# The query/key projection of a transformer layer with x's two parts in one matmul of 512 columns, its halves added at eviction

## The chip, the cores and the metric

The kernel runs on one core of one Trainium2 chip. The metric is the device time of one execution in microseconds (us); a lower time is better. Engines are named as in the profile: PE is TensorE (PEld its weight loads), ACT is ScalarE, DVE is VectorE, POOL is GpSimd, and SPq is SyncE's queue, which issues every DMA here.

## The reference, cut to what matters

One transformer layer on 128 graphs of 128 nodes with 384 features, 8 heads of 48, all in float32, with a per-graph additive bias on the scores; at the end the layer's input is added once more and the rows are normalised.

```python
q = split_heads(x @ wq + bq)
k = split_heads(x @ wk + bk)
v = split_heads(x @ wv + bv)
scores = jnp.einsum('bhqd,bhkd->bhqk', q, k) * scaling   # 48 ** -0.5
scores = scores + attn_bias[:, None, :, :]
attn = jax.nn.softmax(scores, axis=-1)
ctx = jnp.einsum('bhij,bhjd->bhid', attn, v)
attn_out = ctx.transpose(0, 2, 1, 3).reshape(b, n, d) @ wo + bo
x = _rmsnorm(x + attn_out, alpha1, gamma1)
ff = jax.nn.silu(x @ w1 + b1) @ w2 + b2
x = _rmsnorm(x + ff, alpha2, gamma2)
# outside: _layernorm(input + x)
```

## The kernel before

**Groups and slots.** The 128 graphs go in 64 groups of two (PAIR), 256 nodes a group (toks). The program is a row of slots `t`. In one slot four groups are worked on in different stages: group t-1 is projected (`g_proj`), t-2 goes through attention (`g_attn`), t-3 through the first feed-forward product (`g_ff1`), t-4 through the second and the final norms (`g_ff2`), while x of group t is transposed. Slots 4 to 64 hold both a projection and a second feed-forward product: 61 slots of one form. Every engine has its own program with the order written out by hand, and the engines meet through semaphores. Each engine takes its instructions in the order in which they are written; an instruction that waits holds up all that stand behind it on that engine.

**Products.** The large products are made from two parts of each operand, high and low (HI, LO; type fp32r), as three passes: low by high, high by low, high by high. Each pass is one matmul with its own weight load (`passes`, L412).

**The projection of queries and keys** (`project_qk`) makes six blocks of 128 output features, Q0, Q1, Q2 with wq and K0, K1, K2 with wk. A block sums over three parts of the features (kb), three passes each: nine matmuls of 256 columns. PSUM bank ps_work0 takes blocks Q0 and Q1 in its two halves, ps_work1 takes Q2 and K0, and ps_work0 again K1 and K2. `qk_done[n]` tells that bank-filling n (0, 1, 2) is complete. Only filling 2 has to wait for an eviction in the same projection: `qk_ready[0]`, that Q0 and Q1 have been taken out of ps_work0.

**Evictions.** ACT takes out Q0, Q1 (L663), Q2 (L663) and K0 (L666), adding the bias and scaling the queries; DVE takes out K1 and K2 (`keys_out`, L791). They go to qk_flat in SBUF. When all are there (`qk_ready[0..2]`), SPq issues the moves (L345), DMAs that put the heads at their partitions in qk; the scores of the next slot read qk.

**What stands around it in a slot.** PE: scores (L424), `down` (L480, 72 matmuls of 384 columns), then `project_qk`, the transposes of the probabilities (L433), the transposes of x1 (L522, into ps_work0), `project_v(0)`, context (L444, L448), `project_v(1)`, output product (L412, ps_rows), transposes of x, and `up` (L412, 108 matmuls). DVE around the projection: `norm2_and_stats(0)` (L850 to L860), `residual2(1)` (L845), `layer_norm(0)` (L864), `norm2_and_stats(1)`, `layer_norm(1)`, then `keys_out`. ACT: the exponentials, the sum of squares of y for graph 0, a table load (L707), the sum of squares for graph 1 (L645; it waits for `residual2(1)`), and only then `queries_out`. The norms go ACT (sum of squares), POOL (L369, L372, the inverse root), DVE.

**The first slots.** In slot 1 DVE waits for the rows of biases and norm factors (`rows_loaded`) before `keys_out`. In slot 2 (`early`) the projection stands ahead of the scores, and ACT and DVE split weights into high and low parts ahead of its evictions. The loads of later weights stand behind the moves on SPq.

Of the kernel before, what the change touches and what calls it, by code (L numbers as in the profile page):

```python
# [31 lines left out]
ALU = mybir.AluOpType  # L32
# [3 lines left out]
P = 128  # L36
# [13 lines left out]
def build_layer(nc, x, adj, wq, bq, wk, bk, wv, bv, wo, bo, w1, b1, w2, b2,  # L50
# [16 lines left out]
    with ctx:  # L67
# [94 lines left out]

        qk_done, qk_ready = sems("qk_done", 3), sems("qk_ready", 3)
        qk_moved = sem("qk_moved")
# [125 lines left out]
        def _(sp):  # L290
# [23 lines left out]
            def slot_program(t, parity):  # L314
# [24 lines left out]
                if live(g_proj):  # L339
                    if live(g_attn):  # L340
                        sp.wait_ge(scores_done[PAIR - 1], through(g_attn))
                    for i in range(3):
                        sp.wait_ge(qk_ready[i], through(g_proj))
                    for p0, c, to, pair, n in moves:
                        sp.dma_start(qk[to:to + n, :, pair, :], qk_flat[p0:p0 + n, :, c, :]).then_inc(qk_moved, 16)  # L345
# [59 lines left out]
        def _(pe):  # L405
# [78 lines left out]
            def project_qk(g):  # L484
                for i in range(2):
                    pe.wait_ge(xT_lo[i], through(g))
                for n, blocks in enumerate((((wq_s, 0), (wq_s, 1)), ((wq_s, 2), (wk_s, 0)),
                                            ((wk_s, 1), (wk_s, 2)))):
                    if g == 0 and n < 2:
                        pe.wait_ge(weight_split, (n + 1) * kd)  # L490

                    if n == 0 and live(g - LAG_FF1 + LAG_PROJ - 1):
                        pe.wait_ge(silu_ready[fc // 2 - 2], through(g - LAG_FF1 + LAG_PROJ - 1))
                    elif n == 0 and live(g - 1):
                        pe.wait_ge(v_ready[1], through(g - 1))
                    elif n == 1 and live(g - LAG_FF1 + LAG_PROJ - 1):
                        pe.wait_ge(silu_ready[fc // 2 - 1], through(g - LAG_FF1 + LAG_PROJ - 1))
                    elif n == 1 and live(g):
                        pe.wait_ge(xT_lo[0], through(g))
                    elif n == 2:  # L500
                        pe.wait_ge(qk_ready[0], through(g))
                    for j, (w, c) in enumerate(blocks):
                        mm = passes(ps_work[n % 2][:, j * toks:(j + 1) * toks], [
                            (lambda part, kb=kb: w[:, part, kb, c * P:(c + 1) * P],
                             lambda part, kb=kb: xT[:, part, kb, :]) for kb in range(kd)])
                    mm.then_inc(qk_done[n], 1)

            def project_v(g, b):
                if g == 0 and b == 0:
                    pe.wait_ge(weight_split, proj_units)  # L510
                pe.wait_ge(qk_ready[b + 1], through(g))
                if b == 1 and live(g + LAG_PROJ - LAG_FF1):
# [45 lines left out]
            def transpose_x1(g, parity):  # L558
# [3 lines left out]
                if live(g + LAG_FF1 - LAG_PROJ):  # L562
                    pe.wait_ge(qk_ready[2], through(g + LAG_FF1 - LAG_PROJ))
                elif live(g - 1):
                    pe.wait_ge(silu_ready[fc // 2 - 2], through(g - 1))
# [54 lines left out]
        def _(act):  # L620
# [35 lines left out]

            def queries_out(g, n):

                act.wait_ge(qk_done[n], through(g))
                if n == 0 and live(g - 1):  # L660
                    act.wait_ge(qk_moved, through(g - 1, 16 * len(moves)))
                for j, c in enumerate(((0, 1), (2,))[n]):
                    e = act.activation(qk_flat[:, Q, c, :], ps_work[n][:, j * toks:(j + 1) * toks], ACT.Identity,  # L663
                                       bias=bq_col[:, c:c + 1], scale=scale)
                if n == 1:
                    e = act.activation(qk_flat[:, K, 0, :], ps_work[1][:, toks:2 * toks], ACT.Identity,  # L666
                                       bias=bk_col[:, 0:1])
                e.then_inc(qk_ready[n], 1)

# [21 lines left out]
            def slot_program(t, parity):  # L691
# [5 lines left out]
                if early:  # L697
                    weights_hi(t, 0)
                    for n in range(2):
                        queries_out(g_proj, n)  # L700
                if live(g_attn):
# [8 lines left out]
                if live(g_proj) and not early:  # L710
                    queries_out(g_proj, 0)
                    if t == 1:
                        weights_hi(t, 0)
                    queries_out(g_proj, 1)
                if live(g_attn):
# [26 lines left out]
        def _(dve):  # L742
# [41 lines left out]

            def keys_out(g):

                dve.wait_ge(qk_done[2], through(g))
                if live(g - 1):
                    dve.wait_ge(qk_moved, through(g - 1, 16 * len(moves)))
                for c in (1, 2):  # L790
                    e = dve.tensor_scalar(qk_flat[:, K, c, :], ps_work[0][:, (c - 1) * toks:c * toks],  # L791
                                          bk_col[:, c:c + 1], None, ALU.add)
                e.then_inc(qk_ready[2], 1)

# [72 lines left out]
            def slot_program(t, parity):  # L867
# [5 lines left out]
                if early:  # L873
                    weights_lo(t, 0)
                    keys_out(g_proj)
                if live(g_attn):
# [7 lines left out]
                if live(g_ff2):  # L884
                    norm2_and_stats(g_ff2, 0)
                    residual2(g_ff2, 1, parity)
                    layer_norm(g_ff2, 0)
                    norm2_and_stats(g_ff2, 1)
                    layer_norm(g_ff2, 1)
                if live(g_proj) and not early:  # L890
                    keys_out(g_proj)
                if live(g_ff1):
# [54 lines left out]
```

## Time and profile before

| | |
|---|---|
| median of 3 runs | 2987.4 us (2986.91 to 2988.67) |
| the profiled execution | 2988.56 us, of it 2986.8 us span |
| PE busy | 2926.4 us, 98% of the span |
| DVE busy | 1970.5 us, 66% |
| ACT busy | 1443.7 us, 48% |
| POOL busy | 695.6 us, 23% |
| TensorE clock granted, mean over the span | 0.991 |

The profile page gives busy times by engine, the chain of work that ended last, and groups of instructions; the timeline gives instructions in order of time, merged where neighbours are alike. Ends of matmuls are modelled, so a busy PE is not PE at its peak: the spacing of matmuls is read from their starts. In the steady slots `down` starts every 45.42 us.

### The profile page before, as it was taken

How to read it: one execution, taken by the hardware profiler on the slowest of the kernel's cores; microseconds unless marked ns; L12 is line 12 of the kernel's file. 1: busy time of each engine (PE TensorE's matmuls, PEld its weight loads, DVE VectorE, ACT ScalarE, POOL GpSimd, SP SyncE). 2: the span in 40 equal slices, each digit the busy share in tenths (PEclk: the TensorE clock that was granted, in tenths of full speed). 3: DMA queues.
4: the chain of work that ended last, by engine and by line, in shares of the span. 5: the costliest groups of instructions: out<-in, count | busy, mean ns of one | idle time of the engine just before them, and what ended most of it. 6: DMA issues, size and time to landing. Idle time of an engine off the chain costs nothing.

```text
span 2986.8 us, 62755 instructions
## 1 busy us (share of the span) xinstructions
PE 2926.4 (98%) x25216; PEld 2874.6 (96%) x25216; DVE 1970.5 (66%) x3621; ACT 1443.7 (48%) x4263; POOL 695.6 (23%) x968
## 2 busy tenths in 40 slices
PE   6899999999999999999999999999999999999997
PEld 5899999999999999999999999999999999999997
DVE  4666666666666666666666666666666666666664
ACT  4554554544545545544545445455455445454452
POOL 0122222222222222222222222222222222222221
PEclk8999999999999999999999999999999999999998
DMA  5212112112112121121121121121211211211210
GB/s 155 68 47 68 55 47 68 49 54 68 45 58 68 35 68 56 47 68 56 47 68 51 51 68 46 56 68 37 66 56 47 68 56 47 68 52 51 63 38 17
DMA packets 155476, 171.93 MB, mean 58 GB/s; under 512 B 18609, under 2 KB 155185, under 8 KB 155185
## 3 DMA queue, kind: packets, MB, share of 16 engines
q1 hardware_dynamic: 155184, 167.91, 18.8%
q8 instruction: 200, 3.28, 0.5%
q14 instruction: 92, 0.75, 0.1%
HBM read 92.35 MB, written 25.17 MB: 39 GB/s over the span
## 4 chain that ended last, share of the span: by engine, by line
PE 96%; DVE 1%; ACT 1%; SPq 1%; issue 0%; DMA 0%; POOL 0%; POOLq 0%; ACTq 0%; DVEq 0%
PE ps_work L412 48%; PE ps_rows L480 27%; PE ps_rows L412 7%; PE ps_att L424 4%; PE ps_att L433 4%; PE ps_att L444 2%; PE ps_att L448 2%; PE ps_work L522 2%; PE ps_rows L522 1%; ACT probs L630 1%; SPq L302 0%; SPq L345 0%; DMA stage<-in_L_gnn_w 0%; DVE w_s L754 0%; DVE y L864 0%
## 5 line engine op out<-in xcount | busy, mean ns | idle before, releaser
L412 PE MATMUL ps_work<-x1T,w_s 128*128 128x256 f32 x6912 | 848.4, 283 | 8.0 <-DVE x1T L812 7.1
L412 PEld LDWEIGHTS ps_work<-x1T,w_s 128*128 128x128 f32 x6912 | 836.6, 189 | 8.6 <-DVE x1T L812 7.3
L480 PE MATMUL ps_rows<-w_s,h 128*128 128x384 f32 x4608 | 816.1, 338 | 0.0
L480 PEld LDWEIGHTS ps_rows<-w_s,h 128*128 128x128 f32 x4608 | 795.9, 188 | 7.5
L686 ACT ACTIVATE h_raw<-ps_work,b_col 128x256 f32<-128x256 f32 x768 | 321.9, 470 | 485.6 <-PE ps_work L412 485.6
L630 ACT ACTIVATE probs<-probs,neg_max 128x128 f32<-128x128 f32 x1024 | 396.1, 388 | 249.0 <-DVE neg_max L766 249.0
L834 DVE CAST h<-h_raw 128x512 fp32r<-128x512 f32 x384 | 164.7, 429 | 314.5 <-ACT h_raw L686 314.5
L836 DVE TENSOR_TENSOR h<-h_raw,h 128x512 fp32r<-128x512 f32 x384 | 359.5, 936 | 13.2
L369 POOL TENSOR_SCALAR mean_sq<-sum_sq 128x1 f32<-128x1 f32 x256 | 68.8, 269 | 984.7 <-ACT squares L645 984.7
L381 POOL TENSOR_TENSOR x_last<-x_last,rows 128x768 f32<-128x768 f32 x64 | 117.5, 1836 | 773.6 <-PE ps_att L424 773.6
L412 PE MATMUL ps_work<-wv_s,xT 128*128 128x384 f32 x1152 | 235.8, 349 | 2.9 <-DVE qk_flat L791 2.9
L412 PE MATMUL ps_work<-xT,wk_s 128*128 128x256 f32 x1728 | 217.3, 283 | 21.7 <-ACT qk_flat L663 21.7
L412 PEld LDWEIGHTS ps_work<-xT,wk_s 128*128 128x128 f32 x1728 | 210.9, 191 | 22.1 <-ACT qk_flat L663 22.1
L412 PE MATMUL ps_work<-xT,wq_s 128*128 128x256 f32 x1728 | 216.8, 283 | 4.6 <-DVE wq_s L754 2.9
L412 PEld LDWEIGHTS ps_work<-xT,wq_s 128*128 128x128 f32 x1728 | 214.3, 191 | 5.5 <-issue 3.3
L412 PE MATMUL ps_rows<-wo_s,ctxT 128*128 128x384 f32 x1152 | 213.2, 339 | 4.5 <-DVE ctxT L781 4.5
L412 PEld LDWEIGHTS ps_work<-wv_s,xT 128*128 128x128 f32 x1152 | 196.6, 188 | 15.6 <-issue 12.3
L412 PEld LDWEIGHTS ps_rows<-wo_s,ctxT 128*128 128x128 f32 x1152 | 203.2, 190 | 5.1 <-DVE ctxT L781 4.7
L645 ACT ACTIVATE squares<-x 128x384 f32<-128x384 f32 x128 | 67.4, 527 | 281.3 <-DVE x L819 281.2
L630 ACT ACTIVATION_READ_ACCUMULATOR probs<-probs,neg_max 128x1 f32 x1024 | 191.8, 187 | 0.0
L649 ACT ACTIVATE probs<-ps_att 128x1024 f32<-128x1024 f32 x128 | 124.3, 1022 | 136.5 <-PE ps_att L433 136.4
L775 DVE TENSOR_TENSOR probs<-probs,row_inv 128x512 f32<-128x512 f32 x256 | 177.2, 692 | 8.8
(75 smaller groups left out, 3441.7 us busy)
## 6 DMA issues: line engine op xcount, KB each, us to landing
qk<-qk_flat SPq DMA_DIRECT2D x384, 96.0 KB, 2.4
x_in<-in_x SPq DMA_DIRECT2D x64, 384.0 KB, 3.2
x_res<-in_x SPq DMA_DIRECT2D x64, 384.0 KB, 3.9
x_last<-in_x SPq DMA_DIRECT2D x64, 384.0 KB, 3.2
out<-y SPq DMA_DIRECT2D x64, 384.0 KB, 2.5
bias<-in_adj SPq DMA_DIRECT2D x64, 128.0 KB, 3.8
qk<-qk_flat SPq DMA_DIRECT2D x128, 64.0 KB, 2.1
stage<-in_L_gnn_w SPq DMA_DIRECT2D x24, 192.0 KB, 4.0
```

The costliest lines, as they stand in the source:

```text
L381: pool.tensor_tensor(x_last[:], x_last[:], row(GAMMA2), ALU.add).then_inc(x_last_biased, 1)
L412: mm = pe.matmul(ps_out, stationary(sta), moving(mov), start=(i == 0), stop=(i == n - 1))
L424: mm = pe.matmul(ps_att[b][:, at:at + P], qk[p0:p0 + dh, Q, c, b * P:(b + 1) * P], qk[p0:p0 + dh, K, c, b * P:(b + 1) * P], start=True, st ...
L433: mm = pe.transpose(ps_att[b][:, head * P:(head + 1) * P], probs[:, b, head, :], ident[:])
L480: mm = pe.matmul(ps_rows[b][:, 0:d], h[:, sta, m, b * P:(b + 1) * P], w2_s[:, mov, m, :], start=(m == 0 and i == 0), stop=(m == fc - 1 and ...
L522: mm = pe.transpose(ps_out[:, at:at + P], rows_in[:, b, kb * P:(kb + 1) * P], ident[:])
L630: e = act.activation(probs[:, b, head, :], probs[:, b, head, :], ACT.Exp, bias=neg_max[:, b, head:head + 1], accum_out=row_sum[:, b, head: ...
L649: act.activation(probs[:, b].rearrange("p h n -> p (h n)"), ps_att[b][:], ACT.Copy).then_inc(probsT_ready[b], 1)
L686: e = act.activation(h_raw[:, m % 2, j * toks:(j + 1) * toks], ps_work[m % 2][:, j * toks:(j + 1) * toks], ACT.Silu, bias=b1_col[:, 2 * m ...
L775: dve.tensor_tensor(probs[:, b, heads], probs[:, b, heads], row_inv[:, b, heads].unsqueeze(2).to_broadcast([P, hp, P]), ALU.mult).then_inc ...
L834: dve.tensor_copy(hi, h_raw[:, m % 2, :]).then_inc(h_hi[m], 1)
L836: dve.tensor_tensor(h[:, LO, 2 * m:2 * m + 2, :].rearrange("p c n -> p (c n)"), h_raw[:, m % 2, :], hi.bitcast(F32), ALU.subtract).then_in ...
```

## The change

Each of the six blocks now has a bank to itself in turn: ps_work0 for Q0, Q2, K1 and ps_work1 for Q1, K0, K2. For each kb there is one matmul of 512 columns, the high part of the weights against both parts of x (high in columns 0 to 255, low in 256 to 511), and one of 256 columns, the low part of the weights against the high part of x, into the first half. So a block takes six matmuls in place of nine, and 2304 columns as before. The sum of the two halves of the bank is the block.

Eviction has two steps for every block: ACT takes the first half into qk_flat with bias and scale (`projection_half`, signals `qk_half[n]`), and then DVE adds the second half, scaled, to what stands in qk_flat (`projection_out`, signals `qk_ready[n]`). Block n of 2 or more waits for `qk_ready[n - 2]`. The waits of `project_v`, of the transposes of x1 and of the moves are put on the new semaphores. On DVE the six additions are written between the norm steps.

```diff
-                    elif n == 2:
-                        pe.wait_ge(qk_ready[0], through(g))
-                    for j, (w, c) in enumerate(blocks):
-                        mm = passes(ps_work[n % 2][:, j * toks:(j + 1) * toks], [
-                            (lambda part, kb=kb: w[:, part, kb, c * P:(c + 1) * P],
-                             lambda part, kb=kb: xT[:, part, kb, :]) for kb in range(kd)])
+                    elif n >= 2:
+                        pe.wait_ge(qk_ready[n - 2], through(g))
+                    for kb in range(kd):
+                        cols = slice(c * P, (c + 1) * P)
+                        pe.matmul(ps_work[n % 2][:, 0:2 * toks].rearrange("p (a n) -> p a n", a=2),
+                                  w[:, HI, kb, cols], xT[:, :, kb, :], start=(kb == 0), stop=False)
+                        mm = pe.matmul(ps_work[n % 2][:, 0:toks], w[:, LO, kb, cols], xT[:, HI, kb, :],
+                                       start=False, stop=(kb == kd - 1))
                     mm.then_inc(qk_done[n], 1)
...
-                pe.wait_ge(qk_ready[b + 1], through(g))
+                pe.wait_ge(qk_ready[2 * kd - 1 - b], through(g))
...
-            def queries_out(g, n):
+            def projection_half(g, n):
...
+                of, c = divmod(n, kd)
+                act.activation(qk_flat[:, of, c, :], ps_work[n % 2][:, 0:toks], ACT.Identity,
+                               bias=(bq_col, bk_col)[of][:, c:c + 1],
+                               scale=(scale, 1.0)[of]).then_inc(qk_half[n], 1)
...
-                    queries_out(g_proj, 0)
                     if t == 1:
                         weights_hi(t, 0)
-                    queries_out(g_proj, 1)
+                    for n in range(2 * kd):
+                        projection_half(g_proj, n)
...
-            def keys_out(g):
+            def projection_out(g, n):
+
+                dve.wait_ge(qk_half[n], through(g))
+                of, c = divmod(n, kd)
+                dve.scalar_tensor_tensor(out=qk_flat[:, of, c, :], in0=ps_work[n % 2][:, toks:2 * toks],
+                                         scalar=(scale, 1.0)[of], in1=qk_flat[:, of, c, :], op0=ALU.mult,
+                                         op1=ALU.add).then_inc(qk_ready[n], 1)
```

ACT's order in a steady slot, from the last exponentials to the transposed probabilities. Before:

```order
L630 ACTIVATE probs,row_sum<-probs,neg_max 128x128 x16
L645 ACTIVATE squares,sum_sq2<-y 128x384
L707 ACT_TABLE_LOAD
L645 ACTIVATE squares,sum_sq2<-y 128x384
L663 ACTIVATE qk_flat<-ps_work0,bq_col 128x256 x2
L663 ACTIVATE qk_flat<-ps_work1,bq_col 128x256
L666 ACTIVATE qk_flat<-ps_work1,bk_col 128x256
L649 ACTIVATE probs<-ps_att0 128x1024
```

ACT's order at the same place in the changed kernel (its lines are numbered a little differently, L647 is the sum of squares):

```order
L706 ACT_TABLE_LOAD
L647 ACTIVATE squares,sum_sq2<-y 128x384
L665 ACTIVATE qk_flat<-ps_work0,bq_col 128x256
L665 ACTIVATE qk_flat<-ps_work1,bq_col 128x256
L665 ACTIVATE qk_flat<-ps_work0,bq_col 128x256
L665 ACTIVATE qk_flat<-ps_work1,bk_col 128x256
L665 ACTIVATE qk_flat<-ps_work0,bk_col 128x256
L665 ACTIVATE qk_flat<-ps_work1,bk_col 128x256
L651 ACTIVATE probs<-ps_att0 128x1024
```

ACT's four evictions have become six, one a block, still all behind the second sum of squares. DVE's order in a steady slot, from `residual2(1)` on. Before:

```order
L845 TENSOR_TENSOR y<-ps_rows,x 128x384
L864 TENSOR_SCALAR y<-y,mean_var,inv_std 128x384
L850 SCALAR_TENSOR_TENSOR y<-y,inv_rms,rows 128x384
L856 TENSOR_TENSOR y<-y,x_last 128x384
L858 BN_STATS stats<-y 128x6
L860 BN_AGGR mean_var<-stats 128x2
L864 TENSOR_SCALAR y<-y,mean_var,inv_std 128x384
L791 TENSOR_SCALAR qk_flat<-ps_work,bk_col 128x256 x2
```

DVE's order at the same place in the changed kernel (L788 is the addition of a block's second half):

```order
L842 TENSOR_TENSOR y<-ps_rows,x 128x384
L861 TENSOR_SCALAR y<-y,mean_var,inv_std 128x384
L788 SCALAR_TENSOR_TENSOR qk_flat<-ps_work,qk_flat 128x256 x2
L847 SCALAR_TENSOR_TENSOR y<-y,inv_rms,rows 128x384
L853 TENSOR_TENSOR y<-y,x_last 128x384
L855 BN_STATS stats<-y 128x6
L857 BN_AGGR mean_var<-stats 128x2
L788 SCALAR_TENSOR_TENSOR qk_flat<-ps_work,qk_flat 128x256 x2
L861 TENSOR_SCALAR y<-y,mean_var,inv_std 128x384
L788 SCALAR_TENSOR_TENSOR qk_flat<-ps_work,qk_flat 128x256 x2
```

The two evictions of keys behind the norms have become six additions, two by two among the norm steps of graph 1.

## Rows read from the trace of the kernel before

**Rows 1.** The page: busy time by engine, and the chain that ended last.

```profile
PE 2926.4 (98%) x25216; PEld 2874.6 (96%) x25216; DVE 1970.5 (66%) x3621; ACT 1443.7 (48%) x4263; POOL 695.6 (23%) x968
...
PE 96%; DVE 1%; ACT 1%; SPq 1%; issue 0%; DMA 0%; POOL 0%; POOLq 0%; ACTq 0%; DVEq 0%
```

**Rows 2.** Timeline of PE, steady slot: start us, us, engine, line, tiles, count.

```profile
1481.04 12.75 PE L480 MATMUL ps_rows<-w_s,h 128*128 128x384 f32 x72
...
1493.63 3.34 PE L412 MATMUL ps_work<-xT,wq_s 128*128 128x256 f32 x27
...
1496.81 3.33 PE L412 MATMUL ps_work<-xT,wk_s 128*128 128x256 f32 x27
...
1499.97 1.91 PE L433 MATMUL ps_att<-ident,probs 128*128 128x128 f32 x16
...
1507.63 3.28 PE L412 MATMUL ps_rows<-wo_s,ctxT 128*128 128x384 f32 x18
...
1510.75 0.60 PE L522 MATMUL ps_work<-ident,x_in 128*128 128x128 f32 x4
```

**Rows 3.** Timeline of ACT around the same projection.

```profile
1495.56 0.53 ACT L645 ACTIVATE squares<-y 128x384 f32<-128x384 f32 x1 [2.35 <-DVE y L845]
...
1496.08 0.82 ACT L663 ACTIVATE qk_flat<-ps_work,bq_col 128x256 f32<-128x256 f32 x2
1498.06 0.47 ACT L663 ACTIVATE qk_flat<-ps_work,bq_col 128x256 f32<-128x256 f32 x1 [1.16 <-PE ps_work L412]
```

**Rows 4.** Timeline of DVE around the same projection.

```profile
1495.00 0.52 DVE L845 TENSOR_TENSOR y<-ps_rows,x 128x384 f32<-128x384 f32 x1
1496.03 0.48 DVE L864 TENSOR_SCALAR y<-y,mean_var,inv_std 128x384 f32<-128x384 f32 x1 [0.50 <-POOL inv_std L372]
1497.22 0.62 DVE L850 SCALAR_TENSOR_TENSOR y<-y,inv_rms,rows 128x384 f32<-128x384 f32 x1 [0.71 <-POOL inv_rms L372]
...
1499.06 0.18 DVE L860 BATCH_NORM_AGGREGATE mean_var<-stats 128x2 f32<-128x6 f32 x1
...
1500.58 0.87 DVE L791 TENSOR_SCALAR qk_flat<-ps_work,bk_col 128x256 f32<-128x256 f32 x2
```

**Rows 5.** Groups of instructions by form: count, busy us, mean ns of one, idle before.

```profile
L850 DVE SCALAR_TENSOR_TENSOR y<-y,inv_rms,rows 128x384 f32<-128x384 f32 x128 | 79.2, 619 | 94.2 <-POOL inv_rms L372 94.2
...
L856 DVE TENSOR_TENSOR y<-y,x_last 128x384 f32<-128x384 f32 x128 | 71.5, 558 | 4.4
...
L812 DVE TENSOR_TENSOR x1T<-ps_rows,x1T 128x256 fp32r<-128x256 f32 x64 | 26.5, 414 | 0.0
```

**Rows 6.** Timeline, two hand-overs between engines: DVE to PE, then ACT to DVE.

```profile
20.17 0.88 DVE L791 TENSOR_SCALAR qk_flat<-ps_work,bk_col 128x256 f32<-128x256 f32 x2 [4.83 <-DMA rows<-in_L_gnn_gamma]
...
21.10 2.30 PE L412 MATMUL ps_work<-wv_s,xT 128*128 128x384 f32 x9 [2.86 <-DVE qk_flat L791]
...
1502.87 0.60 ACT L673 ACTIVATE x1T<-ps_work 128x512 fp32r<-128x512 f32 x1
...
1503.51 0.69 DVE L812 TENSOR_TENSOR x1T<-ps_work,x1T 128x512 fp32r<-128x512 f32 x1 [2.05 <-ACT x1T L673]
```

**Rows 7.** Timeline of slots 1 and 2: SPq, ACT and PE.

```profile
23.01 7.35 SPq L345 DMA_DIRECT2D qk<-qk_flat  x10
...
40.90 1.19 ACT L663 ACTIVATE qk_flat<-ps_work,bq_col 128x256 f32<-128x256 f32 x3
...
41.77 4.21 PE L412 MATMUL ps_work<-xT,wk_s 128*128 128x256 f32 x18 [9.85 <-ACT qk_flat L663]
45.91 2.16 PE L424 MATMUL ps_att<-qk 48*128 48x128 f32 x32
```

**Rows 8.** Stretches: length, busy us of each engine, PEclk (granted clock), DMA share, GB/s.

```profile
50.00:54.00 4.00, 1.51 (x10) 1.19 (x9) 3.71 (x6) 4.00 (x23) 0.00 (x0) 1.00 0.45 116
54.00:58.00 4.00, 2.02 (x13) 1.79 (x14) 1.74 (x4) 3.97 (x13) 0.00 (x0) 0.80 0.75 198
...
102.00:106.00 4.00, 3.20 (x25) 2.99 (x26) 2.84 (x7) 3.91 (x12) 2.23 (x4) 1.00 0.87 259
```

More of the change, by code:

```diff
@@ L160, in build_layer @@
         xT_lo = sems("xT_lo", 2)
-        qk_done, qk_ready = sems("qk_done", 3), sems("qk_ready", 3)
+        qk_done, qk_half = sems("qk_done", 2 * kd), sems("qk_half", 2 * kd)
+        qk_ready = sems("qk_ready", 2 * kd)
         qk_moved = sem("qk_moved")
@@ L341, in slot_program @@
                         sp.wait_ge(scores_done[PAIR - 1], through(g_attn))
-                    for i in range(3):
+                    for i in range(2 * kd):
                         sp.wait_ge(qk_ready[i], through(g_proj))
@@ L486, in project_qk @@
                     pe.wait_ge(xT_lo[i], through(g))
[L487 to L490, printed above, removed]
+                for n, (w, c) in enumerate([(wq_s, c) for c in range(kd)] + [(wk_s, c) for c in range(kd)]):
+                    if g == 0 and n % kd == 0:
+                        pe.wait_ge(weight_split, n + kd)
                     if n == 0 and live(g - LAG_FF1 + LAG_PROJ - 1):
@@ L562, in transpose_x1 @@
                 if live(g + LAG_FF1 - LAG_PROJ):
-                    pe.wait_ge(qk_ready[2], through(g + LAG_FF1 - LAG_PROJ))
+                    pe.wait_ge(qk_ready[2 * kd - 2], through(g + LAG_FF1 - LAG_PROJ))
                 elif live(g - 1):
@@ L661, in queries_out @@
                     act.wait_ge(qk_moved, through(g - 1, 16 * len(moves)))
[L662 to L668, printed above, removed]
+                of, c = divmod(n, kd)
+                act.activation(qk_flat[:, of, c, :], ps_work[n % 2][:, 0:toks], ACT.Identity,
+                               bias=(bq_col, bk_col)[of][:, c:c + 1],
+                               scale=(scale, 1.0)[of]).then_inc(qk_half[n], 1)
             def transposed_hi(g, i, ps_in, done, xT_out, ready):
@@ L698, in slot_program @@
                     weights_hi(t, 0)
-                    for n in range(2):
-                        queries_out(g_proj, n)
+                    for n in range(2 * kd):
+                        projection_half(g_proj, n)
                 if live(g_attn):
@@ L710, in slot_program @@
                 if live(g_proj) and not early:
-                    queries_out(g_proj, 0)
                     if t == 1:
                         weights_hi(t, 0)
-                    queries_out(g_proj, 1)
+                    for n in range(2 * kd):
+                        projection_half(g_proj, n)
                 if live(g_attn):
@@ L783, in context_lo @@
                                   ALU.subtract).then_inc(ctx_lo[b], 1)
-            def keys_out(g):
[L787 to L793, printed above, removed]
+            def projection_out(g, n):
[4 more added lines that the diff above has]
+                                         op1=ALU.add).then_inc(qk_ready[n], 1)
             def values_out(g, b):
@@ L874, in slot_program @@
                     weights_lo(t, 0)
-                    keys_out(g_proj)
+                    for n in range(2 * kd):
+                        projection_out(g_proj, n)
                 if live(g_attn):
@@ L887, in slot_program @@
                     layer_norm(g_ff2, 0)
+                if live(g_proj) and not early:
+                    for n in range(2):
+                        projection_out(g_proj, n)
+                if live(g_ff2):
                     norm2_and_stats(g_ff2, 1)
+                if live(g_proj) and not early:
+                    for n in range(2, 4):
+                        projection_out(g_proj, n)
+                if live(g_ff2):
                     layer_norm(g_ff2, 1)
                 if live(g_proj) and not early:
-                    keys_out(g_proj)
+                    for n in range(4, 2 * kd):
+                        projection_out(g_proj, n)
                 if live(g_ff1):
```

## The prediction

> **What bounds the kernel now.** I read the page first: PE is busy 98% of the span and makes 96% of the chain that ended last [rows 1], so whatever PE waits in a steady slot is paid in full and nothing on another engine counts unless PE waits for it. Then the timeline of PE in one slot: `down` at 1481.04, the projection at 1493.63, the transposes of the probabilities at 1499.97, with no gap between them [rows 2]. The projection takes 6.34 us for 54 matmuls of 256 columns, 0.1174 us each from start to start; `down` takes 12.59 us for 72 of 384 columns, 0.1749 us each. Last, ACT and DVE in that stretch, because the change puts both between PE and its bank. ACT takes out Q0 and Q1 from 1496.08 to 1496.90, though the bank was filled 18 matmuls after the start, at 1495.74. What keeps it is the sum of squares at 1495.56, which waits for DVE's `residual2(1)`, which starts only at 1495.00 [rows 3, 4]. PE needs the bank again at 1493.63 + 36 x 0.1174 = 1497.86, so today this lateness is hidden with 0.96 us to spare.
>
> **The matmuls.** For each kb and block three matmuls of 256 columns (0.352 us) become one of 512 and one of 256. The trace has none of 512. `down` gives 0.1749 us for 384 columns, and the output product 0.1733 (1507.63 to 1510.75 for 18) [rows 2], so 128 columns more cost 0.0559 to 0.0575 us and 512 columns, by one step more, 0.229 to 0.232. A lower end is 0.224, if the whole difference between 0.117 and 256 columns at 2.4 GHz (0.107) is a fixed part. I take 0.229, between the ends and from the output product, whose 18 matmuls stand in one row: a block is 3 x (0.229 + 0.117) = 1.04 us, six blocks 6.24 us against 6.34. The matmuls alone give back 0.1 us a slot (0.05 to 0.19).
>
> The Trainium skill ("TensorE: Matmul & The Clock Gate", Back-to-back issue gap) gives a matmul its columns over 2.4 GHz plus about 2.5 ns; by it the 18 weight loads and matmuls saved are worth 0.045 us a slot. The trace has 117 ns where that rule has 109, so the measured spacing goes into the sum.
>
> **The evictions, walked through one steady slot** (times as in the slot of rows 2, up to where they move). The new DVE instruction reads PSUM and SBUF, 256 columns, with a scalar. A two-operand one of that size with a PSUM input takes 0.414 us (lower end); with a scalar 384 columns take 0.619 (upper end); the scalar form costs 0.061 us more than the plain one at 384 (0.619 against 0.558) [rows 5]. I take 0.49, nearer the first, since the size is its size. Two independent DVE instructions start 0.08 us closer than one lasts, as L860 and L845, or the pair of L791 (0.87 us for two of 0.48) show [rows 4]. ACT's eviction of 256 columns takes 0.47 us, and two of them 0.82 [rows 3]. Hand-overs: ACT to DVE 0.04 us (1503.47 to 1503.51), DVE to PE 0.05 us (21.05 to 21.10) [rows 6], and from a filled bank to ACT 0.20 us after the next matmul's start (1497.86 to 1498.06) [rows 2, 3].
>
> - Q0 is full at 1494.67, Q1 at 1495.71. ACT is still behind its sum of squares: first halves at 1496.08 to 1496.55 and 1496.43 to 1496.90.
> - DVE adds Q0 from 1496.59 to 1497.08. `layer_norm(0)` ends at 1496.51 and is not in the way [rows 4]. Block 2 (Q2) can start at 1497.13, where PE is ready at 1495.71: **PE waits 1.42 us**. Of this, what was hidden before is used up because the bank is wanted after 12 matmuls instead of 36.
> - DVE adds Q1 from 1497.00 to 1497.49, and so `norm2_and_stats(1)` starts at 1497.41 instead of 1497.22. It ends 0.19 us later than before, at 1499.43 [rows 4]. Behind it stands the addition of Q2.
> - Q2 is full at 1498.17, its first half out at 1498.84; DVE is free for it only from 1499.35, and the addition ends at 1499.84. K1 needs that bank: it starts at 1499.89, while K0 ended at 1499.21. **PE waits 0.68 us**.
> - K0's addition ends at about 1500.40, before K2 wants its bank at 1500.93. K2 ends at 1501.97, where the projection ended at 1499.97 before.
>
> So a slot is 2.00 us longer (1.42 + 0.68 of waits, 0.10 of matmuls back). Nothing behind it is late again: the last additions end at about 1503.2, the transposes into ps_work0 stand behind 16 others that take 1.91 us [rows 2], at about 1503.7, and DVE waited 2.05 us before its next work there [rows 6]. ACT's two additional evictions and DVE's four additional instructions lie inside PE's waits or in idle time; the moves wait for the last addition, some 1.7 us later than for `keys_out` before, and are wanted more than 20 us later, in the next slot. Does the delay repeat? The start of `residual2(1)` hangs on the scores of its own slot (DVE's norms and ACT's exponentials follow them), so the wait is there in each of the 61 slots: **61 x 2.00 = 122 us**.
>
> **Slots 1 to 3.** In slot 1 block 2 now waits for an addition that stands behind DVE's wait for the rows, until 20.17 [rows 6]. Four blocks, partly at the 1.2 GHz level, then end at about 28 us; the moves, which began at 23.01 [rows 7], begin at about 28.8, and with them slip the weight loads behind them and the evictions of slot 2 (40.90): 5.8 us. In slot 2 PE had 18 matmuls left when the eviction came, 4.14 us from 41.77 to 45.91, at the 1.2 GHz level [rows 7], and slot 3 has one more such place, so that there are two; now it has four blocks, some 6.3 us if the clock recovers halfway, and the addition of 0.5 us ahead: 2.6 us more in each. Sum 11 us; 5 if the slip of the moves is hidden, 16 if the four blocks run at that level throughout. The profiled execution took 2988.56 us, 1.2 above the median, and the sum goes on the median: 2987.4 + 122 + 11 = **3120 us**.
>
> **Rivals.**
> - *Only the turn of the bank counts.* If ACT and DVE were at hand, the way round (0.20 + 0.47 + 0.04 + 0.49 + 0.05 = 1.25 us) against the other bank's block (1.04) leaves 0.21 us of wait at four blocks, 0.84 - 0.10 = 0.74 us a slot: 2987 + 45 + 11 = 3043 us. For it: it would hold if the sum of squares came ahead of the projection's start. Against it: ACT is seen at it until 1496.08 [rows 3].
> - *The lag heals itself* (the other side). A longer slot would let DVE and ACT arrive earlier against PE in the next one. If `residual2(1)` came 1.4 us earlier relative to the projection and DVE kept the two waits for POOL clear of it, the matmuls' saving alone would stay: 61 x 0.1, or 6 us, 2981 us, and at most 2992 with the start. It decides at a lead of 1.4 us. Against it: the sum of squares waited 2.35 us for DVE [rows 3], and DVE's work there starts from this slot's scores, not from the last slot.
> - *The clock falls.* Two waits in a slot may bring PE down to 1.2 GHz. In the start, with 1.51 and 2.02 us of work in two stretches of 4, the granted clock went from 1.00 to 0.80; with 3.20 us of work in 4 it stayed at 1.00 [rows 8]. Here the stretch from 1495.7 to 1499.9 would have 2.1 us of work and 2.1 of waits, between these. A fall costs at least what 18 matmuls lose at the lower level, 4.14 - 2.11 = 2.0 us [rows 2, 7]: 61 x 2.0 = 122, or 3242 us. The Trainium skill ("TensorE: Matmul & The Clock Gate", A second HAM failure mode: psum-queue depth-cycling) tells of just this, a kernel whose short idle times at the turn of PSUM banks make the clock swing. Whether pauses of 1.4 and 0.7 us do it, no run here shows yet.
> - *The matmul of 512 is slower than its columns*, as it reads x in two pieces of 256. At 0.26 us each, block 0, 1 and 3 still lie inside the same waits, and only K1 and K2 count: 6 x 0.03 x 61 = 11 us. This lies inside the range.
>
> **How the numbers follow.** The forecast has a chance of 0.80, the fall of the clock 0.10, the turn of the bank alone 0.06, the healing lag 0.04. The forecast's own bounds: with DVE's addition at 0.414 us both waits shrink together by 0.19 us a slot, 12 us; at 0.62 they grow by 0.4, 24 us; the start gives -6 and +5, the long matmul +11. Not all at once: 3092 to 3156 us. The other cases hold 0.20 together and stay outside. Faster or slower by over 0.2% (6 us) is about what a measurement of this kernel can tell from no change: faster 0.03, within 0.01, slower 0.96.
>
> **What would show it.** In a steady slot: PE's projection over about 8.3 us instead of 6.34, with waits for DVE's qk_flat ahead of Q2 (1.4 us) and K1 (0.7 us) and none ahead of K0 and K2; DVE's first addition right behind ACT's first half, which itself starts as its sum of squares ends; `norm2_and_stats(1)` between the second and third additions; slots every 47.4 us. Q2 waiting 0.2 us would speak for the bank's turn alone, no wait for the healing lag, and a granted clock under 1.00 in the steady stretch for the clock. The forecast is wrong if `down` starts every 45.3 us or every 49.

## The result, and the profile after

The changed kernel takes 3110.4 us (median of 4 runs, 3109.3 to 3111.7) where the kernel before, run beside it, takes 2988.0 (median of 4): 122.4 us slower, a ratio of 1.0412 with an interval of 1.0399 to 1.0425. The prediction was 3120 us, range 3092 to 3156.

From the page: busy time by engine and the chain that ended last, against [rows 1].

```profile
PE 2954.0 (95%) x24064; PEld 2818.5 (91%) x24064; DVE 2061.5 (66%) x3877; ACT 1511.5 (49%) x4391; POOL 695.9 (22%) x968
...
PE 56%; DVE 18%; ACT 17%; issue 6%; POOL 2%; DMA 1%; SPq 0%; POOLq 0%; ACTq 0%; DVEq 0%
```

PE has 1152 matmuls fewer, but the chain no longer stays on PE: it goes over ACT and DVE for a third of the span. That share is not the time lost, for PE is still busy 95% of the span: at each of PE's waits the chain turns to what released it and follows that engine's work back, over additions and norm steps to the exponentials (ACT probs L632 alone are 13% of the chain). The way there can be read in one steady slot. Timeline of PE, with the first matmul of each block (Q0, Q1, Q2, K0, K1, K2), against [rows 2]:

```profile
1605.24 0.39 PE L504 MATMUL ps_work<-xT,wq_s 128*128 128x512 f32 x1
1605.47 0.28 PE L506 MATMUL ps_work<-xT,wq_s 128*128 128x256 f32 x1
...
1606.29 0.39 PE L504 MATMUL ps_work<-xT,wq_s 128*128 128x512 f32 x1
...
1608.66 0.50 PE L504 MATMUL ps_work<-xT,wq_s 128*128 128x512 f32 x1 [1.17 <-DVE qk_flat L788]
1608.99 0.28 PE L506 MATMUL ps_work<-xT,wq_s 128*128 128x256 f32 x1
...
1609.81 0.39 PE L504 MATMUL ps_work<-xT,wk_s 128*128 128x512 f32 x1
...
1611.26 0.50 PE L504 MATMUL ps_work<-xT,wk_s 128*128 128x512 f32 x1 [0.25 <-DVE qk_flat L788]
...
1612.41 0.39 PE L504 MATMUL ps_work<-xT,wk_s 128*128 128x512 f32 x1
...
1613.45 1.91 PE L434 MATMUL ps_att<-ident,probs 128*128 128x128 f32 x16
```

An undisturbed block takes 1.05 us (1605.24 to 1606.29). Q2 could start at 1607.33 and starts at 1608.66, 1.33 us late; K1 could start at 1610.86 and starts at 1611.26, 0.40 late. After each wait the step from the first matmul to the second is 0.33 or 0.34 us in place of 0.23; I call this the restart. K0 and K2 do not wait. The projection lasts 8.21 us instead of 6.34.

Timeline of ACT and then of DVE there, against [rows 3, 4]:

```profile
1607.17 0.52 ACT L647 ACTIVATE squares<-y 128x384 f32<-128x384 f32 x1 [2.35 <-DVE y L842]
...
1607.69 0.82 ACT L665 ACTIVATE qk_flat<-ps_work,bq_col 128x256 f32<-128x256 f32 x2
1610.01 0.48 ACT L665 ACTIVATE qk_flat<-ps_work,bq_col 128x256 f32<-128x256 f32 x1 [1.50 <-PE ps_work L506]
```

```profile
1608.18 0.79 DVE L788 SCALAR_TENSOR_TENSOR qk_flat<-ps_work,qk_flat 128x256 f32<-128x256 f32 x2
1608.89 0.61 DVE L847 SCALAR_TENSOR_TENSOR y<-y,inv_rms,rows 128x384 f32<-128x384 f32 x1
...
1610.71 0.18 DVE L857 BATCH_NORM_AGGREGATE mean_var<-stats 128x2 f32<-128x6 f32 x1
1610.81 0.39 DVE L788 SCALAR_TENSOR_TENSOR qk_flat<-ps_work,qk_flat 128x256 f32<-128x256 f32 x1
1611.55 0.42 DVE L788 SCALAR_TENSOR_TENSOR qk_flat<-ps_work,qk_flat 128x256 f32<-128x256 f32 x1 [0.35 <-ACT qk_flat L665]
```

Read it as a relay: the sum of squares keeps ACT until 1607.69, the first half of Q0 goes out, DVE adds from 1608.18, PE starts Q2 at 1608.66. And Q2's first half is out at 1610.49, but DVE is in its norm steps until 1610.8, adds then, and PE starts K1 at 1611.26.

How much this is in all slots stands in one row of each kernel: the 4608 matmuls of `down`, with their first and last start. The first of them is in slot 4, ahead of the first steady projection; between the first and the last lie all 61 steady projections. The kernel before, then the changed one (the columns behind the count are the shortest, median and longest duration in ns, then the first and last start in us):

```profile
L480 PE MATMUL ps_rows<-w_s,h x4608: 333/336/444, 118.3 to 2977.9; 128*128 128x384 f32 x192
```

```profile
L481 PE MATMUL ps_rows<-w_s,h x4608: 335/336/444, 126.4 to 3100.3; 128*128 128x384 f32 x192
```

The start is 8.1 us later; between first and last lie 2973.9 us in place of 2859.6, 114.3 more or 1.874 us for each of the 61. Together 122.4 us, the whole of the difference. The experiments below are read in the same way, as **start** (first of these matmuls against 118.3) and **steady** (excess per projection over 2859.6/61).

The granted clock did not fall: it is 1.00 over the stretch from 126 to 3000 us, which holds the steady slots. Stretches of PE in the waits, columns as in [rows 8]; the first holds Q2's wait, the last is laid from one wait over the other:

```profile
1605.20:1609.20 4.00, 2.83 (x17) 2.26 (x16) 3.33 (x9) 1.34 (x4) 1.58 (x4) 1.00 0.00 0
...
1607.30:1611.30 4.00, 2.58 (x15) 1.87 (x13) 3.40 (x8) 1.94 (x6) 1.38 (x5) 1.00 0.01 3
```

### The profile page after: what moved, and what is told of

It reads as the page before. It is cut to its first block, busy times and chain, and to the rows that moved or that the text cites. A ratio compares the mean times of both kernels' runs of the same rounds, so it can differ in the third digit from the quotient of the medians.

```text
span 3109.3 us, 60837 instructions
## 1 busy us (share of the span) xinstructions
PE 2954.0 (95%) x24064; PEld 2818.5 (91%) x24064; DVE 2061.5 (66%) x3877; ACT 1511.5 (49%) x4391; POOL 695.9 (22%) x968
## 4 chain that ended last, share of the span: by engine, by line
PE 56%; DVE 18%; ACT 17%; issue 6%; POOL 2%; DMA 1%; SPq 0%; POOLq 0%; ACTq 0%; DVEq 0%
PE ps_work L413 34%; ACT probs L632 13%; PE ps_rows L413 6%; PE ps_work L504 4%; PE ps_att L434 4%; DVE neg_max L765 3%; DVE probs L761 3%; DVE y L847 2%; DVE stats L855 2%; DVE y L853 2%; DVE qk_flat L788 2%; PE ps_att L445 2%; PE ps_att L449 2%; PE ps_work L524 2%; ACT h_raw L685 2%
## 5 line engine op out<-in xcount | busy, mean ns | idle before, releaser
L632 ACT ACTIVATE probs<-probs,neg_max 128x128 f32<-128x128 f32 x1024 | 395.8, 388 | 245.0 <-DVE neg_max L765 245.0
L504 PE MATMUL ps_work<-xT,wq_s 128*128 128x512 f32 x576 | 217.0, 411 | 107.9 <-DVE qk_flat L788 103.2
L504 PEld LDWEIGHTS ps_work<-xT,wq_s 128*128 128x128 f32 x576 | 110.0, 191 | 148.5 <-DVE qk_flat L788 123.4
L788 DVE SCALAR_TENSOR_TENSOR qk_flat<-ps_work,qk_flat 128x256 f32<-128x256 f32 x384 | 157.1, 419 | 131.9 <-ACT qk_flat L665 122.8
L504 PE MATMUL ps_work<-xT,wk_s 128*128 128x512 f32 x576 | 216.0, 409 | 15.4 <-DVE qk_flat L788 15.4
L413 PEld LDWEIGHTS ps_work<-wv_s,xT 128*128 128x128 f32 x1152 | 196.6, 188 | 13.8 <-issue 13.7
L647 ACT ACTIVATE squares<-x 128x384 f32<-128x384 f32 x128 | 67.3, 526 | 281.7 <-DVE x L816 281.6
L632 ACT ACTIVATION_READ_ACCUMULATOR probs<-probs,neg_max 128x1 f32 x1024 | 191.8, 187 | 0.0
L396 POOL TENSOR_TENSOR x<-x,rows 128x768 f32<-128x768 f32 x64 | 118.2, 1847 | 288.0 <-PE ps_rows L524 288.0
```

The lines of the kernel that those rows point to most:

```text
L396: pool.tensor_tensor(x1[:, 1 - parity], x1[:, 1 - parity], row(B2), ALU.add).then_inc(x1_b2_ready, 1)
L413: mm = pe.matmul(ps_out, stationary(sta), moving(mov), start=(i == 0), stop=(i == n - 1))
L504: pe.matmul(ps_work[n % 2][:, 0:2 * toks].rearrange("p (a n) -> p a n", a=2), w[:, HI, kb, cols], xT[:, :, kb, :], start=(kb == 0), stop=F ...
L632: e = act.activation(probs[:, b, head, :], probs[:, b, head, :], ACT.Exp, bias=neg_max[:, b, head:head + 1], accum_out=row_sum[:, b, head: ...
L788: dve.scalar_tensor_tensor(out=qk_flat[:, of, c, :], in0=ps_work[n % 2][:, toks:2 * toks], scalar=(scale, 1.0)[of], in1=qk_flat[:, of, c, ...
```

## Experiments

| kernel | median us | ratio to before (interval) | start, us | steady, us a projection |
|---|---|---|---|---|
| the changed kernel | 3110.4 | 1.0412 (1.0399 to 1.0425) | +8.1 | +1.87 |
| e1_dve_order | 3149.1 | 1.0542 (1.0526 to 1.0558) | +5.4 | +2.52 |
| e2_q0_first | 3108.1 | 1.0405 (1.0388 to 1.0422) | +6.7 | +1.84 |
| e3_both_orders | 3085.7 | 1.0331 (1.0315 to 1.0346) | +8.8 | +1.49 |
| e7_e1_keys_before_norm | 3093.4 | 1.0355 (1.0339 to 1.0372) | +6.5 | +1.61 |
| e6_e3_keys_before_norm | 3029.4 | 1.0140 (1.0122 to 1.0158) | +7.5 | +0.57 |
| e4_no_addition | 2984.8 | 0.9991 (0.9981 to 1.0000) | +0.1 | -0.08 |
| e5_rows_wait_later | 3104.7 | 1.0393 (1.0379 to 1.0408) | +2.6 | +1.87 |
| c1_three_passes_spare_bank | 2978.9 | 0.9973 (0.9963 to 0.9983) | -9.4 | 0.00 |
| f1_six_banks | 2973.8 | 0.9958 (0.9945 to 0.9970) | -10.4 | -0.08 |
| f2_six_banks_rows_later | 2975.4 | 0.9960 (0.9946 to 0.9973) | -6.6 | -0.09 |

A start is not known to a microsecond. Up to the first `down`, e1, e2, e3, e6 and e7 have the same order of instructions on every engine as the changed kernel, and yet their starts run from +5.4 to +8.8; a difference of some 3 us between two starts says nothing. The steady part does not have this spread.

The question of the first three: is each wait set by the order on ACT and DVE, so that taking one away only uncovers the next (theory A in the expectations), or are the waits independent?

**e2_q0_first: Q0 ahead on ACT (first piece) and on DVE (second piece).**

```diff
+                if live(g_proj) and live(g_ff2):
+                    projection_half(g_proj, 0)
                 if live(g_ff2):
                     sum_of_squares(g_ff2, 1, y[:, 1, :], res2_ready, sum_sq2, sq2_ready)
...
                     residual2(g_ff2, 1, parity)
+                    if live(g_proj):
+                        projection_out(g_proj, 0)
                     layer_norm(g_ff2, 0)
```

> ACT takes Q0's first half ahead of the second sum of squares, and DVE adds Q0 ahead of the first layer norm; all else as in the changed kernel. Theory A: Q2 starts at about 1607.5 instead of 1608.66 in the slot read, its wait falls from 1.33 to 0.2 us; but the addition of Q2 still stands behind the norm steps, which end when they did, so K1 starts at 1611.2 as before and its wait grows from 0.4 to about 1.5 us. The slot stays at 47.3 us: 3108 to 3110 us. Rival (the two waits are independent and add up): 61 x 1.1 = 67 us less, 3043 us.

Measured 3108.1 us. Its PE timeline, blocks Q2, K0 and K1:

```profile
1557.88 0.50 PE L504 MATMUL ps_work<-xT,wq_s 128*128 128x512 f32 x1
...
1559.03 0.48 PE L504 MATMUL ps_work<-xT,wk_s 128*128 128x512 f32 x1
...
1561.58 0.50 PE L504 MATMUL ps_work<-xT,wk_s 128*128 128x512 f32 x1 [1.25 <-DVE qk_flat L790]
```

The projection starts at 1555.61, so Q2 could start at 1557.70 and is 0.18 us late instead of 1.33. K1 could start at 1560.17 and is 1.41 late instead of 0.40. The two waits are 1.59 us together where they were 1.73, K0 has a slow first matmul too, and the projection lasts 8.17 us against 8.21: the wait moved, as theory A says, and the rival's 3043 us is out.

**e1_dve_order: the additions of Q2 and K0 ahead of the norm steps.**

```diff
                 if live(g_proj) and not early:
-                    for n in range(2):
+                    for n in range(4):
                         projection_out(g_proj, n)
                 if live(g_ff2):
                     norm2_and_stats(g_ff2, 1)
-                if live(g_proj) and not early:
-                    for n in range(2, 4):
-                        projection_out(g_proj, n)
                 if live(g_ff2):
                     layer_norm(g_ff2, 1)
```

> DVE's additions of Q2 and K0 stand ahead of the second norm steps instead of behind them; all else as in the changed kernel. Theory A (each wait is the latest of ACT's and DVE's in-order work): K1 no longer waits for the norm steps but for its bank's own way round; its block starts at about 1611.0 instead of 1611.26 in the slot read, Q2's wait of 1.33 us stays. Slot 47.04 us instead of 47.30, in all 61 x 0.26 = 16 us less: 3094 us. Rival (the bank's turn alone sets the waits, the order does not matter): 3110 us, unchanged.

Measured 3149.1 us, 39 slower than the changed kernel where 16 faster was expected: a miss. PE and then DVE behind the projection:

```profile
1582.16 1.91 PE L434 MATMUL ps_att<-ident,probs 128*128 128x128 f32 x16
1584.78 0.63 PE L524 MATMUL ps_work<-ident,x 128*128 128x128 f32 x4 [0.71 <-DVE qk_flat L788]
```

```profile
1582.69 0.18 DVE L857 BATCH_NORM_AGGREGATE mean_var<-stats 128x2 f32<-128x6 f32 x1
1583.82 0.48 DVE L861 TENSOR_SCALAR y<-y,mean_var,inv_std 128x384 f32<-128x384 f32 x1 [0.95 <-POOL inv_std L373]
1584.22 0.75 DVE L788 SCALAR_TENSOR_TENSOR qk_flat<-ps_work,qk_flat 128x256 f32<-128x256 f32 x2
```

The projection itself (1574.22 to 1582.16) lasts 7.94 us, 0.27 less than in the changed kernel, as expected (K1 starts 1.19 us after K0 instead of 1.45). But the norm steps now run later on DVE, `layer_norm(1)` behind them waits 0.95 us for POOL, and behind that stand the additions of K1 and K2. The transposes of x1 go into ps_work0, K1's bank, and wait: 2.62 us after the transposes of the probabilities, where 1.75 is usual. I had worked the expectation out as far as the end of the projection and not to the next user of the bank.

**e3_both_orders: e1 and e2 together.**

> Both changes of order together. Theory A: Q2 waits 0.2 us, K1 about 0.13, each with 0.1 us of restart, the projection takes about 6.8 us instead of 8.2; slot 45.9 us, in all 61 x 1.4 = 85 us less: 3025 us, of which 8 us over the kernel before are the first slots and 29 us the turn of the bank. Rival (effects add): the sum of what the two gave alone.

Measured 3085.7 us. The projection was near what was expected (6.9 us instead of 8.2), but the same wait of the transposes stood behind it (1553.73, then 1556.36). So the gain was 25 us and not 85. The rival's sum fails too: alone the two gave -2 and +39 us, together -25.

**e6 and e7: the additions of K1 and K2 ahead of `layer_norm(1)`,** on top of e3 and of e1:

```diff
-                if live(g_ff2):
-                    layer_norm(g_ff2, 1)
                 if live(g_proj) and not early:
                     for n in range(4, 2 * kd):
                         projection_out(g_proj, n)
+                if live(g_ff2):
+                    layer_norm(g_ff2, 1)
```

> The kernel with both changes of order, and the additions of K1 and K2 ahead of layer_norm(1) instead of behind it. In its trace K1's addition stood behind a layer norm that waits 0.95 us for POOL, and PE waited for it ahead of the transposes into ps_work0 (2.63 us from the transposes of the probabilities to those of x1, where 1.75 is usual). If that is the whole of what the first expectation missed, the slot falls from 46.92 by 0.88 to 46.04 us and the time from 3085.7 by 61 x 0.88 = 54 us to 3032. Rival (something else behind the projection is late as well, DVE's splits or the values): above 3045 us.

> The kernel with only the second change of order (additions of Q2 and K0 ahead of the norm steps), and the additions of K1 and K2 ahead of layer_norm(1). The wait ahead of the transposes into ps_work0 (2.62 us where 1.75 is usual) goes: slot 47.94 - 0.87 = 47.07 us, 3149.1 - 53 = 3096 us, 15 us under the changed kernel, as was first expected of that change alone. Rival: above 3110 us.

Measured 3029.4 and 3093.4 us, against 3032 and 3096. This settles what the first expectations had missed: to within 3 us it was that one wait. With the order mended, e7's 3093 is also what e1 was first expected to give (3094), and e6's 3029 what e3 was (3025). e6 has the best order with two banks of those run: still 42 us over the kernel before, 0.57 us a projection. Its PE timeline, the first matmuls of Q2, K0 (with its second), K1, K2 and the transposes:

```profile
1520.46 0.50 PE L504 MATMUL ps_work<-xT,wq_s 128*128 128x512 f32 x1
...
1521.60 0.50 PE L504 MATMUL ps_work<-xT,wk_s 128*128 128x512 f32 x1
1521.94 0.28 PE L506 MATMUL ps_work<-xT,wk_s 128*128 128x256 f32 x1
...
1522.79 0.50 PE L504 MATMUL ps_work<-xT,wk_s 128*128 128x512 f32 x1
...
1523.94 0.49 PE L504 MATMUL ps_work<-xT,wk_s 128*128 128x512 f32 x1
...
1525.09 1.91 PE L434 MATMUL ps_att<-ident,probs 128*128 128x128 f32 x16
```

All four blocks start with a slow first matmul, 1.14 to 1.19 us apart where 1.05 is free. The way round (PE, ACT, DVE, PE) takes 0.20 + 0.47 + 0.04 + 0.42 + 0.05 = 1.18 us in these traces and does not fit behind one block. Of the 0.57 us, 0.40 are the four restarts, 0.23 real waits (0.18 ahead of Q2), and 0.07 come back from the matmuls. Not all of it is the turn of the bank: K0's restart hangs on the order too, since ACT takes Q1's first half only at 1520.63, behind the sum of squares, where the bank was full at 1520.28.

**e4_no_addition: the matmuls by themselves.** `projection_out` does nothing, `projection_half` signals `qk_ready[n]`, Q0's half ahead of the sum of squares as in e2.

> The six additions on DVE are left out (the product of the high weights with the low part of x is computed but not added), ACT's first half alone frees the bank, and Q0's stands ahead of the second sum of squares. It prices the fused matmuls by themselves. Theory A: no wait in a steady slot, the projection takes 6 x 1.045 = 6.27 us against 6.34 in the kernel before, slot 45.35 us: 4 us less than the kernel before in the steady slots, about 4 us more in the first ones, 2988 us (2983 to 2993). Rival (the matmul of 512 columns or the finer turn of the bank itself costs time): above 3000 us.

Measured 2984.8 us, at the edge of what can be told from the kernel before, and inside the expectation. A steady projection is 0.08 us shorter than before (0.07 expected); the start costs 0.1 instead of the 4 I had put down. So the fused matmuls are no slower than their columns say, and nothing of the 122 us comes from them; it comes with the way in which the banks are emptied. How much of that is the addition alone e4 does not tell, because it also takes Q0 past the sum of squares. In the changed kernel's slot read above, Q0's first half is out only at about 1608.17, 0.84 us after PE could have started Q2; so most of Q2's wait would have stayed without any addition. This is an estimate from that trace, and no such kernel was run.

**e5_rows_wait_later: the first slot.**

```diff
                 if t == 1:
                     weights_lo(t, 0)
-                    dve.wait_ge(rows_loaded, 16 * n_rows)
...
+                if t == 1:
+                    dve.wait_ge(rows_loaded, 16 * n_rows)
                 if live(g_proj):
                     values_out(g_proj, 0)
```

> In slot 1 DVE waits for the rows of biases only behind the six additions; all else as in the changed kernel. Theory A: block Q2 of slot 1 starts at about 15.6 us instead of 19.82, and the moves and the weight loads behind them follow, so the start gives back about 4 of its 8 us: 3106 us. Rival (the slip of slot 1 is hidden by the weight DMAs): 3110 us.

Measured 3104.7 us, 5.7 less than the changed kernel (4 expected); start +2.6 instead of +8.1, steady part the same. In slot 1 block Q2 starts at 13.86 us in place of 19.82; e5, then the changed kernel:

```profile
13.86 0.50 PE L504 MATMUL ps_work<-xT,wq_s 128*128 128x512 f32 x1 [1.31 <-DVE qk_flat L788]
```

```profile
19.82 0.79 PE L504 MATMUL ps_work<-xT,wq_s 128*128 128x512 f32 x1 [7.54 <-DVE qk_flat L788]
```

So a good part of the start's cost was that PE, in slot 1, came to stand behind DVE's wait for the rows. How large a part is less sure: e5's start is 5.5 us below the changed kernel's, and 2.8 us below the lowest of the starts with the same order.

**f1_six_banks and its control c1.** The four banks of ps_att are idle between the biased scores and the transposes of the probabilities. f1 puts Q0, Q1, Q2, K0 there (pieces: the banks, the waits in `project_qk`, the wait in `transpose_probs`):

```diff
+        def projected(n):
+            return ps_att[n // 2][:, n % 2 * 512:n % 2 * 512 + 512] if n < 4 else ps_work[n - 4][:, 0:512]
...
+                    if n < 4:
+                        if live(g - 1):
+                            if g >= 2:
+                                pe.wait_ge(scores_biased[n // 2], through(g - 1))
+                            else:
+                                pe.wait_ge(qk_ready[n], through(g - 1))
...
-                    elif n >= 2:
-                        pe.wait_ge(qk_ready[n - 2], through(g))
...
+                if g >= 1 and live(g + 1):
+                    for i in range(2):
+                        pe.wait_ge(qk_ready[2 * b + i], through(g + 1))
```

The scores of group 0 get the like wait, and blocks 4 and 5 the waits on ps_work that blocks 0 and 1 had. c1 is the kernel before, three passes and all, with only its first filling in a bank of ps_att.

> The fused matmuls with six banks instead of two: Q0, Q1, Q2, K0 go to the four banks of ps_att, which are free between the biased scores and the transposed probabilities, K1 and K2 to ps_work; evictions and their order as in the changed kernel. Theory A: no bank is used twice in a projection, so no wait; slot 45.35 us, 61 x 0.07 = 4 us under the kernel before, and in slots 2 and 3 PE does the whole projection while ACT splits weights, some 6 us less: 2978 us. Rival (ACT and DVE, with 6 + 6 evictions instead of 4 + 2, delay something behind the projection): above 2990 us.

> Control: the kernel before with its three passes and its evictions, only the first filling (Q0, Q1) goes to a bank of ps_att, so that the third filling need not wait. Theory A: nothing changes in the steady slots (45.42 us), slots 2 and 3 lose the wait ahead of 18 matmuls: 4 to 6 us less than the kernel before, 2983 us. What f1 is below this is the worth of the fused matmuls, about 4 us. Rival (f1's gain is all in the first slots): c1 equals f1.

Measured 2973.8 us for f1 and 2978.9 for c1, both faster than the kernel before. In f1 the projection runs through; PE's first and last block start and the transposes:

```profile
1480.66 0.39 PE L518 MATMUL ps_att<-xT,wq_s 128*128 128x512 f32 x1
...
1485.87 0.39 PE L518 MATMUL ps_work<-xT,wk_s 128*128 128x512 f32 x1
...
1486.91 1.91 PE L444 MATMUL ps_att<-ident,probs 128*128 128x128 f32 x16
```

6.25 us, against 6.34 in three passes. The row of `down` in f1, and then in c1:

```profile
L491 PE MATMUL ps_rows<-w_s,h x4608: 335/336/444, 107.9 to 2962.7; 128*128 128x384 f32 x192
```

```profile
L484 PE MATMUL ps_rows<-w_s,h x4608: 335/336/444, 108.9 to 2968.5; 128*128 128x384 f32 x192
```

Both gain in the start (10.4 and 9.4 us). PE still stops in slots 2 and 3 (in c1 for 10.8 us ahead of slot 2's scores), but by the time that ACT, busy with the weights or the exponentials, has taken Q0 and Q1 out, the whole projection is done. The kernel before had 18 matmuls still to do then, 4.0 to 4.1 us at the 1.2 GHz level. In c1 the scores of slot 2 start at 41.27 instead of 45.91, and the transposes of the probabilities of slot 3 at 80.62 instead of 89.51. Both kernels are 4 us faster than expected; what was put down too small is this start, at 4 to 6 us for c1 and some 6 for f1. In the steady slots c1 is exactly the kernel before, and f1 is 4.8 us under it. So of f1's 13.7 us c1 gives 8.6, nearly two thirds, with one spare bank and three passes, and about 5 us are the fusion (e4's steady part, 4.6 us, says the same). f1 against c1 is 5.1 us by the medians; the two ratios' intervals overlap, so that the traces, 4.8 us of steady part, carry this more than the times do.

**f2_six_banks_rows_later: f1 with e5's change.**

> f1 and, in slot 1, DVE's wait for the rows behind the additions. Theory A: 2 us under f1, 2976 us; if the weight DMAs hide slot 1, the same as f1.

Measured 2975.4 us, not told apart from f1. Its start is 3.8 us later than f1's, hardly more than starts differ by themselves; whether the later wait for the rows does anything here is open.

## Why the prediction was right, point by point

- **The matmuls.** 0.23 us for 512 columns and 1.05 us a block (0.229 and 1.04 were put down); 0.08 us a projection back where 0.10 was expected, seen by itself in e4 and f1.
- **Q2's wait.** 1.33 us against 1.42. The mechanism, ACT's second sum of squares ahead of all evictions and DVE's addition behind them, is shown by e2, which takes Q0 past it and brings the wait to 0.18. The term of the sum that was too large was DVE's addition: 0.42 us and not 0.49. At the place of the walk, DVE's first addition starts when it should (1608.18; the walk shifted to this slot gives 1608.20).
- **K1's wait.** 0.40 us against 0.68. With the shorter additions the norm steps began 0.13 us earlier than in the walk and K1 0.24 us earlier, while K0 ended 0.04 us later; a wait that is the difference of two long stretches takes all of both errors. That it hangs on the norm steps in front is shown by e1 and e7, which take it past them: K1 then starts 1.19 us after K0 instead of 1.45.
- **A cost the walk did not have.** 0.10 us at each restart: the step from the first matmul after a wait is 0.33 us and not 0.23. It stands twice in a slot and filled up part of what the two waits were short. (The one at Q2 only makes K1's wait shorter, since DVE sets K1's start; the one at K1 lengthens the slot.) The two errors, an addition put too long and a restart left out, have opposite signs, and that they partly cancel is luck; either alone would have left the forecast inside its range. So a slot is 1.33 + 0.40 + 0.20 - 0.07 = 1.86 us longer (measured 1.87, predicted 2.00), and the 61 slots 114 us instead of 122.
- **Slots 1 to 3.** 8.1 us against 11. The part of slot 1 was right in kind: e5's start is 5.5 us lower. What was put too large is the slip that it hands on, 5.8 us: ACT's first eviction of slot 2 starts at 45.00 instead of 40.90, 4.1 us later. Slot 2 adds 2.2 us up to its scores (52.20 instead of 45.91), near the 2.6 put down; 0.9 of the 6.3 us is made up by slot 3's projection (74.58 instead of 69.18), slot 3 adds 3.2, more than the 2.6 (its transposes of the probabilities start at 98.10 instead of 89.51), and 0.5 is made up by the first `down`. With starts that differ by 3 us on their own, 8.1 against 11 is no finer a test than that.
- **The range.** Its lower end, 3092 us, does not follow from its terms: the addition at 0.414 us and the hidden slip take 12 and 6 us off 3120, which gives 3102. And an addition 0.076 us shorter comes three times on the way to K1, so both waits shrink by 0.23 us, 14 us in all, and not by 0.19. The measured 3110 lies inside either way.
- **The rivals.** The lag does not heal (the slot read is 1.87 us longer and so is the mean of the 61), and the turn of the bank nearly alone is what e6 has, 3029 us where this rival was priced at 3043. The clock stayed at 1.00, also in the stretch of 4 us with 2.58 us of work. The matmul of 512 columns is no slower for reading x in two pieces (0.23 us, in e4 and f1 as well). The rule on clock swings at the turn of PSUM banks, cited from the Trainium skill ("TensorE: Matmul & The Clock Gate", A second HAM failure mode: psum-queue depth-cycling), does not show here.

## What to carry to other kernels

A bank of PSUM that is wanted again one block after it was filled (1.05 us here) instead of two (2.11 us) must be emptied within that block's time, and by engines whose order was written when there was time to spare; before splitting an eviction over two in-order engines, walk the way from the last matmul through both to the next user of that bank, and go on to the user after that. When a wait is taken away, look for the next one before counting the gain: here one change of order moved the wait (2 us gained), another uncovered a third (39 us lost), and most of the gain, 81 us, came only with all of them together. And ask first whether PSUM has idle banks at that hour: six banks in place of two turned 4.1% slower into 0.4% faster, most of which the old three passes could have as well.

## What the runs showed of the hardware

- After a wait of PE on DVE's addition the first matmul of 512 columns is 0.33 to 0.34 us from the next instead of 0.23, ahead of Q2 and K1 in all 61 steady slots of the changed kernel. No idle time need be seen for it: in e6 K0 and K2 start 0.06 to 0.08 us after the addition that frees their bank ends, straight behind the block before, and their first step is still 0.32 to 0.34 us. In e1 K2 starts 0.16 to 0.18 us after that end, and its first step is 0.23.
- From the end of DVE's addition to the start of PE's matmul that waited for it pass 0.05 to 0.06 us, in all these slots.
- DVE's instruction with an immediate scalar, one operand in PSUM and one in SBUF, takes 0.42 us for 256 columns, the same as the plain two-operand form (0.41). The 0.06 us that the scalar form costs more at 384 columns [rows 5] belongs to an instruction whose scalar is read per partition and whose operands are both in SBUF; which of these makes the difference was not separated.
- A matmul of 512 columns that reads its moving operand in two pieces of 256, with a weight load before it, follows the line of 256 and 384 columns: 0.117, 0.173, 0.23 us.
